# Linear attention on one core: another order of the same work on TensorE, ScalarE and VectorE

## What is computed

```
h = _ln(x, g1, beta1)
q = _phi((h @ wq).reshape(b, s, H, DH), proj)     # H = 16 heads of DH = 64
k = _phi((h @ wk).reshape(b, s, H, DH), proj)     # _phi(x) = elu(x @ proj) + 1
v = (h @ wv).reshape(b, s, H, DH)
kv = kv + k_t[..., :, None] * v_t[..., None, :]   # for each token t, in order
ksum = ksum + k_t
out = einsum(q_t, kv) / (einsum(q_t, ksum) + 1e-06)
x = x + outs @ wo
```

## Time and profile before

| | |
|---|---|
| median of 3 runs | 2047.44 us (2046.84 to 2049.26) |
| the profiled execution | 2051.5 us |
| its span in the trace | 2049.7 us |
| TensorE matmul busy, whole span | 1692.7 us (83%) |
| TensorE weight loads busy | 943.6 us (46%) |
| VectorE / ScalarE / GpSimd busy | 1413.4 us (69%) / 1060.3 us (52%) / 519.6 us (25%) |
| granted TensorE clock, mean | 0.945 |
| linear attention, TensorE | from 1011.30 us (first features) to about 1559 us of the span |

### The profile page before, as it was taken

One profiled execution on the slowest core, in us unless ns is written; L12 is line 12 of the kernel. 1 busy time (PEld: TensorE's weight loads), 2 busy tenths in 40 slices (PEclk: granted clock), 3 DMA queues, 4 the chain that ended last, 5 costly groups with the idle time before them and its releaser, 6 DMA issues. The chain is left out here.

```text
span 2049.7 us, 36773 instructions
## 1 busy us (share of the span) xinstructions
PE 1692.7 (83%) x12704; PEld 943.6 (46%) x12781; DVE 1413.4 (69%) x4005; ACT 1060.3 (52%) x1727; POOL 519.6 (25%) x579
## 2 busy tenths in 40 slices
PE   3788888889998899887599999989997867778566
PEld 1333333333333333322366666666665645546454
DVE  6677777688777787773266666666665488655786
ACT  1466666656666666666344444434442444333453
POOL 5455555553233312300100000000001422200222
PEclk9899999999999999999799999999999977799898
DMA  5334232222222112200000000000000000000000
GB/s 95 56 61 95 62 66 51 45 45 43 48 48 34 27 36 47 47 2 1 0 2 2 2 1 2 2 3 1 2 2 1 1 0 0 1 0 0 6 16 21
DMA packets 56690, 49.82 MB, mean 24 GB/s; under 512 B 9220, under 2 KB 54468, under 8 KB 56516
## 3 DMA queue, kind: packets, MB, share of 16 engines
q1 hardware_dynamic: 53692, 46.45, 12.2%
q10 hardware_dynamic: 2824, 1.11, 0.4%
HBM read 7.10 MB, written 2.10 MB: 4 GB/s over the span
## 5 line engine op out<-in xcount | busy, mean ns | idle before, releaser
L500 ACT ACTIVATE at_probs<-ps 128x1024 f32<-128x1024 f32 (+1 forms) x448 | 427.4, 962 | 280.3 <-PE ps L613 274.2
L757 DVE TENSOR_REDUCE at_M<-ps 128x1 f32<-128x512 f32 x512 | 336.7, 686 | 111.1 <-PE ps L589 110.3
L589 PE MATMUL ps<-at_KS,at_QS 96*128 96x512 bf16 (+3 forms) x1024 | 322.4, 352 | 53.7 <-DVE at_M L752 20.9
L752 DVE CUSTOM_DVE_ANT_0 at_masked<-ps,at_mask_row 128x384 bf16<-128x384 f32 (+3 forms) x512 | 228.9, 486 | 75.7 <-PE ps L589 73.6
L630 PE MATMUL ps<-at_probs,at_V 128*9 128x512 f32 (+3 forms) x2048 | 232.8, 527 | 27.5 <-ACT at_C L508 12.3
L613 PE MATMUL ps<-at_QS,at_KS 128*128 128x512 bf16 x947 | 242.2, 342 | 14.4 <-DMA at_QS<-at_nmT 6.6
L589 PEld LDWEIGHTS ps<-at_KS,at_QS 96*128 96x128 bf16 x1024 | 91.8, 99 | 334.8 <-DVE at_M L757 150.9
L1245 DVE SCALAR_TENSOR_TENSOR la_phiq<-ps,la_ezq 128x512 f32<-128x512 f32 x64 | 44.3, 691 | 146.5 <-ACT la_ezq L1097 146.5
L380 POOL TENSOR_SCALAR_AFFINE_SELECT at_probs<-at_probs 128x256 f32<-128x256 f32 (+1 forms) x192 | 93.5, 489 | 181.1 <-ACT at_probs L500 180.1
L613 PEld LDWEIGHTS ps<-at_QS,at_KS 128*128 128x128 bf16 x1024 | 93.1, 99 | 81.5 <-issue 26.1
L839 POOL TENSOR_TENSOR la_rstd<-la_vare,mhalf 128x4 f32<-128x4 f32 x16 | 16.1, 1008 | 435.8 <-DVE la_vare L834 435.8
(11 more groups left out here) (258 smaller groups left out, 3394.9 us busy)
## 6 DMA issues: line engine op xcount, KB each, us to landing
at_QS<-at_splitq SPq DMA_DIRECT2D x288, 64.0 KB
at_KS<-at_splitk SPq DMA_DIRECT2D x279, 64.0 KB
out<-X SPq DMA_DIRECT2D x8, 256.0 KB, 2.3
at_QS<-at_nmT ACTq DMA_DIRECT2D x64, 8.0 KB
at_KS<-at_splitk ACTq DMA_DIRECT2D x9, 64.0 KB
w_raw<-fp_weights SPq DMA_DIRECT2D x1, 560.0 KB, 5.6
w_wv<-L_attn_a_wv SPq DMA_DIRECT2D x1, 512.0 KB, 6.9
w_wo<-L_attn_a_wo SPq DMA_DIRECT2D x1, 512.0 KB, 6.5
```

The source lines that it names most:

```text
L500: act.activation(v(probs[u % 4][:]), v(src), ACT.Exp, scale=layers[layer(n)]["scale"])\
L589: last = pe.matmul(ps[:, FIRST + U % 2, o * stride:o * stride + width], QS[n % 2][0:SHIFT_AT, h, qt * P:(qt + 1) * P], KS[n % 2][0:SHIFT_A ...
L752: last = v.tensor_tensor_reduce(masked[U % 4][:, o * stride:o * stride + width], src[:, o, :], mask_row[:, 512 - width:512], 1.0, 4 * NEG, ...
L757: v.tensor_reduce(M[gq % 2][:, heads[0]:heads[-1] + 1, qt], src, AX.X, ALU.max).then_inc(max_free, 1)
```

## The change

The strings of order change on three engines, and ScalarE's relu becomes a part of its own (`reluq`, `reluk`), so that it may stand apart from its exponential. No instruction is added or removed.

```diff
@@ steps
+                   "reluq": [(new[0], "reluq", new[1])], "reluk": [(new[0], "reluk", new[1])],
@@
-    STEP = steps("ktok phiq attnT phik va scores state out vb y rest")
+    STEP = steps("phiq attnT phik ktok scores state out va y vb rest")
@@ scalar
+        def below_zero(a):
+            def part(n, j, par, m):
+                act.wait_ge(z_ready, 2 * (PAIRS * n + j) + a + 1)
+                act.activation(below[a][:], ps[:, PHI + a, :], ACT.Relu, scale=-1.0).then_inc(below_ready, 1)
+            return part
+
         def features(a):
             def part(n, j, par, m):
-                u = 2 * (PAIRS * n + j) + a
-                act.wait_ge(z_ready, u + 1)
-                act.activation(below[a][:], ps[:, PHI + a, :], ACT.Relu, scale=-1.0).then_inc(below_ready, 1)
-                act.wait_ge(below_ready, u + 1)
+                act.wait_ge(below_ready, 2 * (PAIRS * n + j) + a + 1)
                 act.activation(ez[a][:], below[a][:], ACT.Exp, scale=-1.0).then_inc(ez_ready, 1)
             return part
@@
-        walk(act, {"hT": new_hT, "v": values, "phiq": features(0), "phik": features(1),
-                   "ktok": new_Ktok, "attnT": new_attnT}, steps("ktok attnT phiq va phik vb"))
+        walk(act, {"hT": new_hT, "v": values, "reluq": below_zero(0), "reluk": below_zero(1),
+                   "phiq": features(0), "phik": features(1), "ktok": new_Ktok, "attnT": new_attnT},
+             steps("reluq attnT phiq ktok reluk phik va vb"))
@@ vector
-             steps("phiq scores state phik chain out rest"))
+             steps("phiq scores state out phik chain rest"))
```

## The result

The changed kernel takes 2022.68 us (median of 4 runs, 2019.09 to 2025.24) against 2047.14 us for the kernel before (4 runs, 2044.53 to 2049.26): a ratio of 0.9878, 95% interval 0.9858 to 0.9898, 24.5 us less. The forecast was 2025.4 with a range from 2016 to 2036.

A forecast was written before the change was run, and what follows sets the result against it. TensorE was taken to bound linear attention, losing time to VectorE's late quotients; six items (13.8 us), the last item (6.2) and first item with fill (2) total 22 us, from 2047.44 to 2025.4, range 2016 to 2036.

The forecast's parts named there:

- The step without `v`: Linear attention step with no `v` matmul: 6.9 to 7.0 us in place of 7.92, 7.86 and 8.23.
- step 1: Second step of an item: put at 7.1 us, a gain of 0.75, with `ln1` on VectorE's way to the masks.
- Step 3: Step behind VectorE's layer norm work: `attnT` waits 1.1 to 1.3 us, 9.8 us against 9.25, a loss of 0.55.
- Steps with `v`: Steps already at TensorE's own pace: a loss of 0.05 us each, 0.2 together per item.
- One item: One of linear attention's eight items, 67.2 us before: 2.3 us less from its steps' gains and losses.
- The last item: Linear attention's final item, without `v` or layer norm: 7 steps from 7.83 to 6.95 us each, 6.2 us gained.
- First item and fill: Start of linear attention: one feature matmul (0.86 us) and the same step gains, 2 us (ends 0 and 4).
- six items at 2.3 us: The linear attention items between 1082.45 and 1491.02, each gaining 2.3 us: 13.8 us.
- Rival 1: In linear attention only TensorE's marked idle time comes back: 14 us gained, measured near 2034; chance 0.15.
- Rival 2: Moves cancel: steps without `v` wait at `phik` for VectorE's key feature; gain 5 us or less, near 2044; chance 0.06.
- Rival 3: Slower: `state` on TensorE waits for ScalarE's `Ktok` copy in 64 steps; 2057 us if 0.9 late; chance 0.05.
- Rival 4: More comes back: layer norm step doesn't pay, `va` entry to scores shrinks; 30 us in all, 2017; chance 0.06.

The follow-up runs named there:

- the second: The changed kernel, unaltered, timed again beside the follow-up experiments: 2018.31 us against 2045.01 for the kernel before, ratio 0.9857.

## Why the prediction was right

- **What bounds the stage**: TensorE at its own pace but for VectorE's late results. Shown from both sides: VectorE's order alone makes the other result late (+14 us), TensorE's alone leaves the quotients late (-3 us), both together gain 25.
- **The step without `v`**: 6.9 to 7.0 us expected, 6.92 to 6.98 measured. The gain in step 1 was 0.88 us for my 0.75: what I had charged to `ln1` did not come, steps 0 and 1 both take 6.98. The wait of `y` for the state copies is left at some 0.05 us in both (`y` at 1090.75, the copies end at 1090.70), too small to be marked.
- **Step 3**: 9.8 expected, 9.69 measured; the wait at the output transposes is 0.89 us and 1.1 to 1.2 in the loop, I had 1.1 to 1.3.
- **Steps with `v`**: a loss of 0.05 each expected, 0.11 measured (8.82 against 8.71 for two `v`) in straight code, 0.04 in the loop (8.69 against 8.65), both in the ends given.
- **One item** in the straight part of the program: from scores to scores 67.18 and 67.22 us before, 64.92 and 64.85 after, 2.3 us less as forecast, and made up as forecast but for small shifts: steps 0 to 2 win 0.94, 0.88 and 1.31, step 3 loses 0.44, steps 4 to 7 lose 0.42 together (0.2 forecast).
- **The last item**: 6.95 us a step expected, 6.94 measured; 6.2 us.
- **The sum in the trace** is off by size: 29.2 us for my 22. From 1082.45 to 1491.02 before is 408.6 us, from 1077.79 to 1468.14 after 390.4: 18.2 us where I had 13.8. First item and fill gave 3.9 (from 1011.30 and 1010.49 to the heads above: 71.2 and 67.3 us), where I had 2. The tail gave another 0.9 (29.2 less the other three). The mis-sized term is "six items at 2.3 us": four of the six run in the looped part of the program, and the steps there are not like the straight ones. From scores to scores, an item without the turn of the loop took 67.6 us before and 64.4 after, 3.2 us less (one, next to the straight code, 2.8); the item with the turn won 4.4, of which 1.3 lie in the step of the turn. I had read one straight item and multiplied.
- **Against the medians** the forecast was 2.7 us too high in the first measurement; in the second the gain was 26.7 us for my 22. That the first came so near is partly luck. The two profiled executions agree outside the stage (1494.0 and 1493.9 us), so their difference is the stage's 29.2, while the medians show 24.5. Before's profiled execution stood 4.1 us above its median; with one trace of it, it isn't shown whether its stage or the rest was the longer one.
- **Rival 1**, that only marked idle comes back (14 us), did not hold in its number: steps 0 to 2 won 3.1 us and not the 2.8 of their marked waits, and step 3 lost 0.44 and not 1.3. But its base was better than I made it. Over the stage the marked waits fell from 38.2 us (the three rows for VectorE above and 0.7 us more) to 12.8 (8.5, 1.6, 1.2 and 1.5 in two smaller rows), 25.4 of the 29.2. The 5 us an item that I read from starts (by the steps as listed it is 4.5: 3.6 in steps 0 to 2 and 0.9 in step 3) were an upper bound of which 2.3 came back. The Trainium skill ("Perfetto Trace Analysis", "Identifying the Most-Contended Engine") calls matmul busy time a poor measure of the room that is left. By matmul busy time TensorE stands at 98.5% now (64.03 of 65.00), by weight loads at 70%; for this change of order the marked waits came nearer to what it gave than either share.
- **Rival 2**, that the moves cancel, did not hold: VectorE's key feature is ready 0.43 us early, and I had 0.2.
- **Rival 3**, the slower one, exists as a mechanism at 0.34 us a step when the key copy is put last; in the changed kernel the copy is 0.49 us early.
- **Rival 4**, more comes back (30 us in all), has the size of the stage's 29.2 and of the looped items' 3.2, but not the mechanism: step 3 does pay, and the steps with two `v` got no shorter.

## What to carry to other kernels

When engines work through fixed orders, write out one steady step with the start of each instruction on all of them, and ask of each result how long before its use it is ready; here a move gained only when the producer's and the consumer's order changed together, and one without the other cost 14 us. Put work that covers a copy (the output projection) between two uses of a single buffer; it was worth 23 us. A block of side work on the helping engine costs when it is longer than that engine's spare time in the step: cut it to fit (4 us in the stage, 6 by the medians).

Read steps and items in each part of the program that runs them, the looped one too, before multiplying. And compare the changed stage itself between traces: the stages that nobody touched differed by up to 8.5 us between executions here.

## What the runs showed of the hardware that I had not expected

The same step runs at another pace in the looped part of the program, at a granted clock of 1.00 in both. In the kernel before, steps with two `v` take 8.72 us in straight code and 8.65 in the loop, while the first two of an item are slower there (8.02 and 7.93 us from scores to scores, 7.86 in straight code). In the changed kernel a step with two `v` takes 8.82 us in straight code and 8.69 to 8.70 us in the loop; in the straight one the distances after both feature matmuls are 0.94 us, in the looped one 0.86 (timeline of TensorE; `attnT`, `phik`, `ktok` behind the `phiq` of 1117.18 above). Straight:

```profile
1118.12 0.63 PE L1204 MATMUL ps<-ident,la_attn 128*128 128x128 f32 x4
1118.59 1.02 PE L1148 MATMUL ps<-la_hT,la_wk 128*128 128x512 f32 x2
1119.53 0.52 PE L1156 MATMUL ps<-ident,la_phik 128*128 128x128 f32 x3
```

In the loop, with its `phiq`:

```profile
1238.18 1.02 PE L1148 MATMUL ps<-la_hT,la_wq 128*128 128x512 f32 x2
1239.04 0.65 PE L1204 MATMUL ps<-ident,la_attn 128*128 128x128 f32 x4
1239.53 1.02 PE L1148 MATMUL ps<-la_hT,la_wk 128*128 128x512 f32 x2
1240.39 0.54 PE L1156 MATMUL ps<-ident,la_phik 128*128 128x128 f32 x3
```

Neither has a marked wait. The cause was not looked for and stays open. The turn of the loop, once in the stage, leaves TensorE idle for 2.6 us in the changed kernel (the row "issue" among its waits above) and 3.4 us before, at the head of a step.
